# GpSimd's scaling of rotated q and k, moved one slot on, in a fused scan, SSM and local-attention kernel

## The reference, cut to what matters

```python
q = l2norm(q) * qs            # over the 64 channels of a head, 8 heads
k = l2norm(k) * ksc
q, k = rotary_xpos(q, k)      # q * cos * scale + rotate_half(q) * sin * scale
o = local_attention(q, k, v)  # windows of 64 tokens, each looks at itself and the one before
```

## Time and profile before

| what | value |
|---|---|
| median of 3 runs | 4382.27 us (4371.91 to 4396.6) |
| the profiled execution's own time | 4383.26 us |
| its span in the profile | 4381.5 us |
| TensorE busy | 3443.4 us (79%) |
| ScalarE busy | 2566.7 us (59%) |
| VectorE busy | 2494.5 us (57%) |
| GpSimd busy | 1723.7 us (39%) |
| mean granted TensorE clock | 0.927 |

### The profile page before, as it was taken

One profiled execution on the slowest core, in us unless ns is written; L12 is line 12 of the kernel. 1 busy time (PEld: TensorE's weight loads), 2 busy tenths in 40 slices (PEclk: granted clock), 3 DMA queues, 4 the chain that ended last, 5 costly groups with the idle time before them and its releaser, 6 DMA issues. The chain is left out here.

```text
span 4381.5 us, 55085 instructions
## 1 busy us (share of the span) xinstructions
PE 3443.4 (79%) x16064; PEld 1847.8 (42%) x16160; DVE 2494.5 (57%) x4239; ACT 2566.7 (59%) x5827; POOL 1723.7 (39%) x1428
## 2 busy tenths in 40 slices
PE   5787888777878787887878787787787787877776
PEld 1244344444434444344443444434444444444443
DVE  5655655656565554665556656565565656656433
ACT  4455556565665655556555565656656565565554
POOL 2353442534334353343533425344243443435332
PEclk9799999999999999999999999999999999989998
DMA  2000000000000000000000000000000000000000
GB/s 79 3 1 1 5 1 6 1 1 6 1 6 1 1 6 1 6 1 1 6 1 6 1 6 1 1 6 1 6 1 1 6 1 6 1 1 3 1 3 3
DMA packets 18384, 20.52 MB, mean 5 GB/s; under 512 B 768, under 2 KB 17152, under 8 KB 17792
## 3 DMA queue, kind: packets, MB, share of 16 engines
q1 hardware_dynamic: 18048, 16.44, 1.1%
HBM read 12.24 MB, written 4.19 MB: 4 GB/s over the span
## 5 line engine op out<-in xcount | busy, mean ns | idle before, releaser
L1428 POOL TENSOR_TENSOR hc<-hst,Cs 128x512 f32<-128x512 f32 x512 | 654.5, 1278 | 1242.0 <-DVE hst L1198 1203.9
L1198 DVE TENSOR_TENSOR_SCAN hst<-dA,bank 128x512 f32<-128x512 f32 x512 | 624.8, 1220 | 323.1 <-ACT dA L893 147.8
L548 PE MATMUL bank<-W,xs 128*128 128x512 f32 x960 | 515.5, 668 | 136.6 <-DVE tmp L1339 133.0
L522 PE MATMUL bank<-hc,C 128*128 128x512 f32 x1024 | 583.8, 656 | 31.5 <-POOL hc L1428 31.5
L899 ACT COPY Cs<-bank 128x512 f32<-128x512 f32 x512 | 298.3, 583 | 307.5 <-PE bank L535 274.2
L1190 DVE TENSOR_TENSOR bank<-u,bank 128x512 f32<-128x512 f32 x512 | 351.5, 686 | 208.5 <-PE bank L535 206.5
L1487 POOL TENSOR_TENSOR oT<-tmp 128x512 f32<-128x512 f32 x256 | 324.4, 1267 | 347.5 <-DVE tmp L1339 196.4
L1502 POOL TENSOR_TENSOR Pm<-Pm,rinv 128x512 f32<-128x512 f32 x256 | 271.0, 1059 | 425.3 <-DVE rinv L1352 406.0
L1024 ACT ACTIVATE Pm<-bank,mx 128x128 f32<-128x128 f32 x1024 | 363.0, 372 | 125.5 <-DVE mx L1359 125.5
L893 ACT ACTIVATE dA<-delta,neg_a 128x512 f32<-128x512 f32 x512 | 370.9, 724 | 44.6 <-DVE hst L1198 43.6
L535 PE MATMUL bank<-parts,sel 96*128 96x512 bf16 x1024 | 338.4, 410 | 74.1 <-issue 30.2
(11 more groups left out here) (220 smaller groups left out, 5996.8 us busy)
## 6 DMA issues: line engine op xcount, KB each, us to landing
W<-wpack SPq DMA_DIRECT2D x1, 4498.0 KB, 13.8
x_tok<-x SPq DMA_DIRECT2D x16, 256.0 KB, 2.9
out<-xa SPq DMA_DIRECT2D x16, 256.0 KB, 2.2
rot<-tables SPq DMA_DIRECT2D x2, 512.0 KB, 16.6
wc_f<-taps SPq DMA_DIRECT2D x1, 1024.0 KB, 19.4
C<-cpack SPq DMA_DIRECT2D x1, 721.0 KB, 15.0
Pm<-mask SPq DMA_DIRECT2D x1, 320.0 KB, 15.3
tmp<-rowpack SPq DMA_DIRECT2D x1, 256.0 KB, 17.5
```

Source lines behind the costliest of these rows:

```text
L522: mm(y_acc[:, :], ident, hc[:, k % 2, :], start=(k == 0), stop=(k == 2 * NS - 1))\
L548: mm(b[:, :], weights, rhs, start=True, stop=True).then_inc(full(ring, job), 1)
L1198: v.tensor_tensor_scan(o, a, b, 0.0, ALU.mult, ALU.add).then_inc(sem("a_h"), 1)
L1428: g_.tensor_tensor(hc[:, k % 2, :], hst[:, k % 2, :], Cs[:, k % 2, :], ALU.mult)\
```

## The change

GpSimd's sums keep their slots, 0 to 3. The scaling of tile s moves from slot s to slot s + 1, where it stands behind the sums of tile s + 1 (in slot 4 there are none). The waits are those of the moved instructions: `t_r` of their own tile, and GpSimd's own last instruction. TensorE's, ScalarE's, VectorE's and SyncE's programs are unchanged.

```diff
                                 g_.tensor_tensor(qtok[:, 2 * kind + s % 2, :], tmp1[:, kind, :], tmp2[:, kind, :], ALU.add)\
                                     .then_inc(sem("t_sum"), 1)
                                 prior.append(step("t_sum", i, k + 1))
-                            pool.wait_ge(*step("t_r", i, 4 * l + s + 1))
+                        if 1 <= s < 1 + NT:
+                            at = s - 1
+                            pool.wait_ge(*step("t_r", i, 4 * l + at + 1))
                             for kind in range(2):
-                                k = 8 * l + 2 * s + kind
+                                k = 8 * l + 2 * at + kind
                                 pool.wait_ge(*prior[-1])
-                                tok = qtok[:, 2 * kind + s % 2, :].rearrange("p (h d) -> p h d", h=HA)
-                                g_.tensor_tensor(tok, tok, over(rqk[:, s, kind, :], DH), ALU.mult).then_inc(sem("t_qk"), 1)
+                                tok = qtok[:, 2 * kind + at % 2, :].rearrange("p (h d) -> p h d", h=HA)
+                                g_.tensor_tensor(tok, tok, over(rqk[:, at, kind, :], DH), ALU.mult).then_inc(sem("t_qk"), 1)
                                 prior.append(step("t_qk", i, k + 1))
```

## The result

The changed kernel is slower, and by twice what was predicted. Its four runs have a median of 4486.32 us (4467.85 to 4505.64), the kernel before 4389.44 us in its four: ratio 1.0213, 95% interval 1.0187 to 1.0239. The same kernel run again with the experiments gave 4492.19 against 4393.18 us, ratio 1.0216 (1.0189 to 1.0244). That is +97 us where +49 was forecast, and it lies outside the range (4405 to 4466).

A forecast was written before the change was run, and what follows sets the result against it. No engine is full; the time is set by four in-order queues waiting for one another. Tile 2's delay, 22.8 + 32.6 us, less 6.7 won, gives +48.7 on 4383.26: 4432 us, range 4405 to 4466.

The forecast's parts named there:

- Where the narrow place is: Slot 4: TensorE's transposes of tile 2, ahead of the first scores, start right after GpSimd's scaling of that tile.
- Tile 2, the price of the wait: Its scaling takes tile 3's place, so transposes and first scores start later: +22.8 us in layer 0, +32.6 in layer 1.
- Tiles 0 and 1: Their later scaling costs nothing; tile 1 has some 0.2 us of cover in layer 1, over 1 us in layer 0.
- Tile 3: Its scaling in slot 4 could make the second scores 1.9 us later; the possible 4 us were not counted.
- What is won: No wait for `rqk`; in layer 1 slot 1's scaling and VectorE's small instructions end earlier: 15 passes of 0.45, -6.7 us.
- Does it stay: Tile 2's delay holds three queues and is counted whole, with nothing swallowed by the softmax units behind.
- (b): Rival: the price is partly given back, the softmax units swallowing half, 4407 us; 9%.
- (c): Rival: no change, 4383 us, the delay swallowed wholly because the time runs through VectorE's scan; 9%.
- (d): Rival: faster, 4345 us; the wait for `rqk` set the pace and 38.7 us go with nothing paid; 4%.
- The clock: TensorE's low clock around the new wait: could add 21 us in layer 0 or give 16 back in layer 1.
- Rival (a): The clock or the second scores cost on top: 4453 and 4, up to 4475 if low stretches reach the next units; 12%.
- nearer bound: The forecast's upper bound, 4453 us, with low-clock stretches adding 21 us in 16 layer 0 passes.

The follow-up runs named there:

- e2: Kernel before the change, with only tile 2's scaling late, behind tile 3's sums in slot 3, tile 3's scaling right behind it; 4486.95 us, ratio 1.0223.
- e1: Changed kernel, with each slot's scaling of the previous tile put ahead of the sums instead of behind them; 4398.99 us, ratio 1.0022.
- e5: Changed kernel, with tile 2's scaling in slot 3 put between the sums of tile 3's q and k; 4409.1 us, ratio 1.0034.
- e8: Changed kernel with bf16 matmuls in TensorE's wait for tile 2's scaling: 2 and 1 in layer 0, 4 and 1 in layer 1; 4448.59 us, ratio 1.0143.
- e6: Kernel before the change, with bf16 matmuls added in waits that TensorE already has there; 4381.63 us, ratio 0.9970.
- e4: Changed kernel with bf16 matmuls in TensorE's wait for tile 2's scaling: 5 and 2 in layer 0, 9 and 2 in layer 1; 4447.75 us, ratio 1.0128.
- e3: Kernel before the change, with only tile 0's scaling late, behind tile 1's sums, tile 1's scaling right behind it; 4392.26 us, ratio 0.9998.
- e7: The changed kernel again without edit, timed beside the kernel before the change; 4492.19 us, ratio 1.0216.
- e10: Changed kernel with no added matmuls, only TensorE's wait for the transposes' bank put ahead of its wait for the scaling; 4476.9 us, ratio 1.0200.
- e11: Changed kernel with 5 bf16 matmuls (9 in layer 1) just behind the transposes of k of tile 2, none in the wait; 4541.94 us, ratio 1.0344.

## Why the prediction was right or wrong

*Where the narrow place is: right.* TensorE's wait for tile 2's scaling in slot 4; e2 shows it alone, e1 and e5 take it away.

*Tile 2, the price of the wait: right in mechanism, near in size.* It is +1.5 us in a full-clock layer 0 pass (predicted 1.5 to 1.6 at the maximum). In the layer 1 pass shown it is +1.6 from scaling to maximum where 2.04 was worked out, since the first scores took 1.43 us at a partly low clock where they had 1.92. With work in the wait the whole change costs 1.28% of 4393, 56 us (interval 48 to 64), the forecast 49. In e8, with half the work, the first maximum comes 1.5 us later in layer 0 and 1.6 in layer 1; the forecast comes to 1.4 and 1.6. But the filling also took away low clock that the kernel before had in layer 1. Against e6, which lacks it too, e4 is 1.6% slower, 69 us. So the wait at full clock is worth 56 to 69 us, part of it perhaps the filling itself, which no run separates.

*Tiles 0 and 1: right, nothing.* *Tile 3: right.* The second scores come 1.9 us later (their mask at 31.79 us behind the first sum, against 29.86), yet e2 without that delay is no faster.

*What is won: right in place, 0.45 us a pass in layer 1;* its 7 us are below what the runs tell, and e3 gave the gain back to another product.

*Does it stay: right.* Nothing was swallowed; rivals (b), (c) and (d) fall. The distance between batches grew by 5.4 us where 3 was forecast.

*The clock: this step failed.* The sum has the clock at zero. Behind that stood two terms: up to 21 us that low stretches would add in layer 0, and 16 us that layer 1 would give back because its low stretches would fall into the new wait. Nothing was given back. The eight products of the first scores took 1.72 us on average in layer 1, where they had 1.73; full clock in them was left in no pass, where three had it. In layer 0 they took 1.40 instead of 1.11 (1.50 in e7). Kept at work in the wait (e4), TensorE did them in 1.05 us in all 32 passes, and the time fell by 32 to 39 us. Some 12 of these e6 finds in the kernel before as well, so the low clock that the change brought cost about 20 to 27 us in place of zero, and the wait 7 to 20 more than its 49. By the mean clocks 640 us at the low level became 786 to 844 (e7), and e4's filling brought them to 648.

Where in a pass all of this is lost stays open. Between the start of tile 2's k scaling and the first maximum e4 is 0.4 us shorter than the changed kernel in layer 0 and 1.3 in layer 1, 27 us in all. Behind the first maximum of layer 1 the changed kernel loses 1.2 us more up to the next pass (2.8 in e7). The low clock among the last softmax units, shown above, is not a good reason for it: between the fourth and the eighth maximum of layer 1 the profiles have 1.5 us of it a pass in the kernel before and 3.9 in the changed one, but 5.6 in e4, 4.4 in e6 and 4.3 in e5, which are all faster than the changed kernel.

Rival (a), with 12%, had the true mechanism in its clock half, and it was sized too low as well (4453 to 4475; measured 4486 and 4492).

The Trainium skill (TensorE: Matmul & The Clock Gate, Part 1) says that the throttled state is the default and activity releases it. The runs agree: work in the wait raised the mean clock from 0.913 (e10) to 0.927 (e4), and in e11 the scores behind the added work ran at 2.4 GHz. The prediction cited the page, named 4453 as the nearer bound by it, and still put the clock at zero.

## What to carry to other kernels

In in-order queues, ask for each moved instruction who waits for it, and measure the distance to that one's start: here 0.2 us of cover stood against a move of two products, 2.2 us. A wait added to TensorE in a busy stretch cost its length here, 56 to 69 us, and then the clock, 20 to 39; price both, and don't count on low clock that is there already to give something back. Some cheap matmuls in the wait bought the second part back.

## What the runs showed of the hardware

Half the filling, 3 and 5 bf16 matmuls of 128x512 in a wait of about 2 us, was as good as 7 and 11 (1.0143 and 1.0128, clock 0.927 in both). With the work just behind the wait the mean clock stayed at 0.913, and the nine matmuls of layer 1 took 2.7 to 4.0 us.

Three of VectorE's instructions over 16 columns end with the GpSimd product beside them: line 1237 takes 0.76 us in the kernel before, and 0.30 where the product ended earlier, in 15 of 16 batches each; line 1250 takes 0.90 us in e3 against 0.18; line 1242 takes 0.90 in all of them. In the first batch, where no product is beside them, each takes 0.17 to 0.18. GpSimd's own scalings stayed between 1042 and 1070 ns. The Trainium skill (GPSIMD Engine Reference, section 1, Specifications) has this contention for VectorE instructions in a 2-port mode or with two SBUF inputs. The trace agrees for lines 1242 and 1250, which have two. Line 1237 has one, and no run shows its mode.
